# An attention and FFN kernel: two additions moved to ACT, y channel-major, deeper rings, new orders

## What is computed

```python
h = layernorm(x)
q, k, v, g = h @ Wq.T, h @ Wk.T, h @ Wv.T, h @ Wg.T          # q, k turned by RoPE, 8 heads of 16
kv, ksum, vsum = einsum(k, v), k.sum(tokens), v.sum(tokens)
num = q @ kv * scale + vsum
den = q @ ksum * scale + S                                   # S: the token count
o = (num / den + conv5(v) + conv_bias) * g                   # depthwise conv of 5 taps over tokens
x = x + o @ Wo.T
y = fp8(bf16(layernorm(x)) / s_in) @ fp8(kernel / s_k) * (s_in * s_k)
out = x + (bf16(y) + bias)                                   # y and bias in bf16
```

## Time and profile before

| what | us |
|---|---|
| median of three runs (lowest, highest) | 173.91 (173.37, 174.36) |
| the profiled execution | 173.71 |
| its span, first instruction to last | 171.9 |
| PE busy | 153.9 |
| DVE busy | 150.1 |
| POOL busy | 136.3 |
| ACT busy | 126.3 |

### The profile page before, as it was taken

One profiled execution on the slowest core, in us unless ns is written; L12 is line 12 of the kernel. 1 busy time (PEld: TensorE's weight loads), 2 busy tenths in 40 slices (PEclk: granted clock), 3 DMA queues, 4 the chain that ended last, 5 costly groups with the idle time before them and its releaser, 6 DMA issues.

```text
span 171.9 us, 3695 instructions
## 1 busy us (share of the span) xinstructions
PE 153.9 (90%) x1052; PEld 124.9 (73%) x1052; DVE 150.1 (87%) x281; ACT 126.3 (73%) x342; POOL 136.3 (79%) x163
## 2 busy tenths in 40 slices
PE   7789999999899999979999999997999799987620
PEld 2378898877688888858887989857787587965400
DVE  2279899999999999978999999969999959999663
ACT  3757783697889888598889798856798686583851
POOL 1436988858989999969889898969499796979970
PEclk9999999999999999999999999999999999999985
DMA  4932022133133616131552552341508050323223
GB/s 126 280 84 61 4 63 80 44 63 95 31 122 95 185 31 185 34 122 34 153 124 68 144 128 74 72 131 36 123 2 214 5 129 26 97 60 93 66 64 114
DMA packets 29286, 15.74 MB, mean 92 GB/s; under 512 B 9680, under 2 KB 26960, under 8 KB 29264
## 3 DMA queue, kind: packets, MB, share of 16 engines
q1 hardware_dynamic: 28688, 15.22, 33.9%
q10 hardware_dynamic: 576, 0.26, 0.6%
HBM read 5.25 MB, written 4.19 MB: 55 GB/s over the span
## 4 chain that ended last, share of the span: by engine, by line
DVE 23%; PE 22%; DMA 17%; issue 14%; POOL 10%; SPq 7%; ACT 5%; DVEq 0%; POOLq 0%; ACTq 0%
DMA xs<-_attn_hidden_states_dram 6%; DVE acc L995 6%; DMA h2T<-h 5%; DMA q_swapped<-q_turned 5%; DVE k_turned L980 4%; PE bank L1305 4%; DVE x L1047 3%; PE bank L1287 3%; DMA w_raw<-in_L_attn_Wo_dram 3%; POOL rs L671 3%; PE bank L1279 3%; DVE st L958 2%; ACT h L451 2%; PE bank L1269 2%; POOL ob L730 2%
## 5 line engine op out<-in xcount | busy, mean ns | idle before, releaser
L995 DVE SCALAR_TENSOR_TENSOR acc<-bank,conv_w,acc 128x510 f32<-128x510 f32 (+1 forms) x48 | 34.7, 722 | 0.1
L393 ACT ACTIVATE h<-xs,nmr,rs 128x128 f32<-128x128 f32 x64 | 26.3, 483 | 1.7 <-POOL nmr L663 1.5
L451 ACT ACTIVATE h<-x,nmr,rs 128x128 bf16<-128x128 f32 x60 | 24.7, 482 | 3.9 <-POOL nmr L674 3.3
L660 POOL TENSOR_TENSOR rs<-ve,minus_half 128x4 f32<-128x4 f32 (+1 forms) x17 | 16.7, 981 | 10.0 <-ACT ve L384 10.0
L671 POOL TENSOR_TENSOR rs<-ve,minus_half 128x4 f32<-128x4 f32 (+1 forms) x17 | 16.6, 978 | 8.7 <-ACT ve L442 8.6
L700 POOL TENSOR_TENSOR qT<-q_turned,q_swapped 128x512 f32<-128x512 f32 x16 | 20.4, 1277 | 3.4 <-DMA q_swapped<-q_turned 3.4
L1343 PEld LDWEIGHTS bank<-w_o,oT 128*128 128x128 f32 x128 | 16.3, 191 | 7.8 <-issue 4.0
L707 POOL TENSOR_TENSOR k<-k_turned 128x512 f32<-128x512 f32 x16 | 20.4, 1275 | 1.8 <-DVE k_turned L980 1.8
L716 POOL TENSOR_TENSOR acc<-acc,outer 128x508 f32<-128x508 f32 x16 | 20.3, 1271 | 0.6 <-DVE acc L995 0.6
L980 DVE TENSOR_TENSOR k_turned<-bank,turn_k 128x1024 f32<-128x1024 f32 x16 | 19.5, 1218 | 1.3 <-PE bank L1269 1.3
L1305 PEld LDWEIGHTS bank<-v,k 128*128 128x128 f32 x128 | 16.6, 190 | 4.4 <-issue 2.9
(11 more groups left out here) (90 smaller groups left out, 338.3 us busy)
## 6 DMA issues: line engine op xcount, KB each, us to landing
q_swapped<-q_turned SPq DMA_DIRECT2D x32, 128.0 KB, 2.8
xs<-_attn_hidden_states_dram SPq DMA_DIRECT2D x15, 256.0 KB, 3.2
out_dram<-ob SPq DMA_DIRECT2D x15, 256.0 KB, 2.9
xs<-_attn_hidden_states_dram SPq DMA_DIRECT2D x2, 128.0 KB, 2.8
turn_q<-in_turn_q_dram SPq DMA_DIRECT2D x1, 256.0 KB, 4.1
turn_k<-in_turn_k_dram SPq DMA_DIRECT2D x1, 256.0 KB, 4.3
out_dram<-ob SPq DMA_DIRECT2D x2, 128.0 KB, 1.8
h2T<-h SPq DMA_TRANSPOSE x14, 2.4
```

The source lines that it names most:

```text
L393: last = nc.scalar.activation(h[:, s, t], xs[:, u % NX, t], ACT.Identity, scale=rs1[:, s, t:t + 1], bias=nmr1[:, s, t:t + 1])
L451: last = nc.scalar.activation(h2[:, s, t], x2[:, u % 3, t], ACT.Identity, scale=rs2[:, s, t:t + 1], bias=nmr2[:, s, t:t + 1])
L995: nc.vector.scalar_tensor_tensor(out=part, in0=p_vT[:, :, lo + off:hi + off], scalar=conv_w[:, k:k + 1], in1=part, op0=ALU.mult, op1=ALU.a ...
```

## The change

The parts:

1. The token count is added to the denominators on ACT (`add_tokens`, new line L461, one instruction a unit), and not on DVE, for units 0 to 14; unit 15 keeps DVE. `den` gets two buffers.
2. For units 0 to 13 the FFN's matmul is turned round: the weights `fwq` are the stationary operand and the rounded h2T the moving one, one matmul of 512 columns; y comes with channels on the partitions. ACT scales it (`move_y`, L537) and adds the bias, now one number a partition (`add_bias` on ACT, L545), and a new DMA transpose (`turn_yc`, L296, issued by SP) brings it back to tokens on the partitions for `final_sum`. POOL's `add_bias` stays for unit 14. The bias is loaded once more as a column.
3. Rings: `NX` 4 to 6; q_turned, q_swapped, k, qT, h2, h2T, ob 2 to 3; x2 3 to 4. The new ybT and ycT have two.
4. PSUM banks are given out anew, so what each PE call waits for is another's release.
5. All lists of calls are in a new order.

```diff
-NX = 4
+NX = 6
+            def turn_yc(u):
+                s = u % 2
+                sp.wait_ge(ycT_done, count(u))
+                if u >= 2:
+                    sp.wait_ge(ob_done, count(u, 2))
+                sp.dma_start(yc[:, s], ycT[:, s], transpose=True).then_inc(yc_in[s], 16)
+            def add_tokens(u):
+                act.wait_ge(num_filled, count(u))
+                if u >= 2:
+                    act.wait_ge(rden_done, count(u, 2))
+                nc.scalar.activation(den[:, u % 2], p_num[:, :, D:NW], ACT.Identity,
+                                     bias=tokens[:, 0:1]).then_inc(den_done, 1)
...
+                nc.scalar.activation(ybT[:, u % 2], p_y[:], ACT.Copy, scale=ysc[:, 0:1]).then_inc(yb_done, 1)
+
+            def add_bias(u):
+                act.wait_ge(yb_done, count(u))
...
+                nc.scalar.activation(ycT[:, u % 2], ybT[:, u % 2], ACT.Identity,
+                                     bias=fb_act[:, 0:1]).then_inc(ycT_done, 1)
...
             def final_sum(u):
                 s = u % 2
-                pool.wait_ge(yc_done, count(u))
-                pool.wait_ge(ob_free[s], 16 * (u // 2) + 16)
+                if u < POOL_Y:
+                    pool.wait_ge(yc_in[s], 16 * (u // 2 + 1))
...
             def invert(u, j=None):
                 part = part_of(j, TPU)
-                dve.wait_ge(num_filled, count_last(u, j=j))
-                nc.vector.tensor_scalar(den[:, part], p_num[:, part, D:NW], float(S), None,
-                                        ALU.add).then_inc(den_done, 1)
                 dve.wait_ge(den_done, count_last(u, j=j))
...
                 def products(q):
+                    if u < POOL_Y:
+                        last = nc.tensor.matmul(p_y[:], fwq[:], q, start=True, stop=True)
```

More of the change, by code:

```diff
@@ new lines, in _ @@
+            add_bias(0)
+            var_eps1(6)
+            norm2(2)
+            conv_outer(5)
+            conv_middle(5)
+            norm1(6)
+            move_y(1)
+            add_tokens(4)
+            move_hT(6)
+            var_eps2(3)
+            quantise_if_small(2, is_small)
+            add_bias(1)
+            move_v(6)
+            norm2(3)
+            var_eps1(7)
+            conv_outer(6)
+            conv_middle(6)
+            norm1(7)
+            quantise_if_small(3, is_small)
@@ L570, in _ @@
+            move_hT(8)
             var_eps2(5)
             move_y(4)
[L572 removed]
+            add_bias(4)
             for t in range(9, 12):
[L574 removed]
                 move_v(t - 1)
                 var_eps1(t)
+                norm2(t - 4)
+                conv_outer(t - 1)
                 conv_middle(t - 1)
[L578 removed]
+                norm1(t)
                 quantise_if_small(t - 4, is_small)
[L580 removed]
+                add_tokens(t - 2)
+                move_hT(t)
@@ L581, in _ @@
                 var_eps2(t - 3)
                 move_y(t - 4)
-                move_hT(t)
-            norm2(8)
+                add_bias(t - 4)
             move_v(11)
             var_eps1(12)
+            norm2(8)
+            norm1(12)
             conv_outer(11)
@@ L623, in _ @@
             var_eps2(12)
+            norm2(11)
+            quantise_if_small(10, is_small)
+            move_v(15)
             norm2(12)
-            move_v(15)
-            quantise_if_small(12, is_small)
+            add_tokens(14)
+            move_y(10)
+            quantise_if_small(11, is_small)
+            add_bias(10)
             conv_outer(15)
@@ L769, in _ @@
+            final_sum(1)
             sum_outer(5)
-            add_k(6)
             pow2(4)
-            add_bias(3)
-            final_sum(3)
             add_q(6)
             pow1(8)
+            final_sum(2)
+            add_k(7)
             sum_outer(6)
-            for t in range(9, 12):
-                add_k(t - 2)
+            final_sum(3)
+            pow2(5)
+            add_q(7)
+            pow1(9)
+            final_sum(4)
+            add_k(8)
+            for t in range(10, 12):
+                sum_outer(t - 3)
@@ L1465, in _ @@
+            transpose_t1(5, (t2_done, count_last(4)))
+            transpose_v(7, (tap_done[-1], count(6)))
+            project_g(5, (v_done, count(7)))
+            project_k(7, (yb_done, count(3)))
+            sum_v(6, (t1_done, count_last(5)))
+            project_o(5, (q_turned_done, count(7)))
+            attend(6)
+            transpose_h(8, (oT_done, count_last(5)))
+            ffn(4, is_small, (k_turned_done, count(7)))
+            for t in range(9, 12):
                 key_value(t - 2, (kvs_done, count(t - 3)))
-                transpose_t1(t - 3, (hT_done, count_first(t - 1)))
```

847 lines of the change are left out of this document (457 added, 390 removed).

## The result

The changed kernel takes 177.68 us (median of 4 runs, 176.42 to 179.97), the kernel before 173.64 (173.28 to 174.36) on the same chip. The longest execution, 179.97, counts as one in a slower state and is left out of the ratio, which is 1.020 (95% interval 1.012 to 1.028; the median of the other three is 177.11). I had forecast 171.4 and given 168.0 to 177.0, so both the sign and the range were wrong. The profile is of that longest execution, 2.3 us over the median; it shows where time goes, and the medians show how much. Ratios to before are given with their 95% intervals throughout.

What follows compares the result with a forecast made beforehand. PE and DVE were taken as full, with steps of 8.79 and 8.72 us. Start 46.3, ten steps 86.5 plus 3.3 of losses, tail 24.1 and end chain 9.2 gave 169.4, plus 1.8 and 0.2: 171.4 us, range 168.0 to 177.0.

Steps and rivals of the forecast that it cites:

- The start: Start to unit 5's turning of h: 46.3 us against 47.46, from two FFNs coming later and 0.68 us of waiting gone.
- The ten steps: Unit 5's to unit 15's turning of h: 86.5 us bare plus 3.3 of losses, against 92.24 before.
- 3.3 of losses: In the ten steps: 1.0 for the loop through ACT's move of hT, 1.2 a late landing, 1.1 ACT's full queue.
- SP had room: SP's queue: new transposes land in 2.4 us each with 1.2 of SP's time, which it has to spare.
- No wait of DVE for x after 60 us: Sign in the profile after: six x buffers take away the wait at 114.55 us and its like.
- 1.6 us more cover: Rounding in the steps, now behind norm1: 1.6 us more cover for the transpose, which takes 2.4 to 4.1.
- ACT's full queue: Loss in the ten steps: between 0 and 4.75 us, taken as 1.1 because three buffers let ACT run ahead.
- The end: From unit 15's turning: 24.1 us to the last variance, then an unchanged 9.2 end chain.
- My rival in which POOL's sums give the gain back: Tail: POOL's sums of units 11 and 12 delay the last powers; 2.5 us, total 173.9, no change; chance 0.16.
- ACT as the bound: Rival for the ten steps: ACT's waits stay, step 9.75 us, total 178.0, or 174.4 with half the waits; chance 0.22.
- Its first sign: Sign of ACT as the bound: turnings of h between units 5 and 12 lie 9.3 to 9.75 us apart.
- The shared port: Rival for the end: a DVE instruction held by POOL's third sum costs 0.9 us, total 172.3; chance 0.05.

Runs made afterwards that it cites:

- weights rounded early: Changed kernel with POOL's rounding of the FFN weights back behind add_q(1), not behind add_k(3): 173.92 us, ratio to before 1.0004.
- two orders more: Changed kernel, FFN weights rounded at the old place, h2 of units 2 and 8 turned ahead of y, load of x for unit 10 earlier: 171.54 us, ratio 0.987.
- h2 turned first: Changed kernel, FFN weights rounded at the old place, h2 of unit 2 turned ahead of x's load for unit 8 and y's transpose: 172.65 us, ratio 0.989.
- changed kernels of the table: Profiles of the changed kernel, the one with weights rounded early and the one with two orders more; unit 15 to end 32.1, 32.3 and 32.4 us.
- rounding late in before: Kernel before with only the rounding of the FFN weights moved behind add_k(3): 181.13 us, ratio 1.043.
- y not turned: Changed kernel without its part 2: no transpose of y, no bias on ACT, bias on POOL ahead of each final sum: 184.44 us, ratio 1.058.
- tokens on DVE: Changed kernel without its part 1, FFN weights still rounded late: token count added on DVE ahead of the reciprocal: 177.11 us, ratio 1.019.
- wait filled: Changed kernel with 13 matmuls of zeros on PE ahead of project_q(4), FFN weights still late: 176.42 us, ratio 1.011.
- part 2 in the old order: Kernel before with part 2 of the change added and nothing else moved: 184.89 us, ratio 1.058.
- before with the deeper ring: Kernel before with six x buffers in place of four and the load of x for unit 13 issued earlier: 171.55 us, ratio 0.988.

## Why the prediction was wrong

**The start: the step that failed.** I put unit 5's turning at 46.3, from three small gains, and let every other move in the head pass at no cost. The move of `round_ffn_weights` was in the diff; I asked what POOL had to spare there, not who waits for the weights and what stands behind that wait. DVE's wait for `w_ready` is in both kernels at the same place, ahead of `residual(1)`, and PE needs that residual's bank. It came at 51.49. With the call back in place it is 46.19, so the rest of the term was right. In medians this step is 3.8 us (177.68 less 173.92) of the 6.3 by which the forecast was off, or 3.2 of 5.7 without the longest execution. I had named it only in the last sentence, "if the new order of the head costs more than its 1.1 gain", without a size or a place; as a rival it would have had one: 3.8 us of POOL work ending 13 us later.

**The ten steps: mis-sized, and one wait overlooked.** Bare 86.5 and 3.3 of losses were forecast. With the weights rounded early the losses were 7.1 (93.59), with the two orders more 4.6 (91.14). They are of two kinds.

The first is single late transfers from SP's order, as before the change: h2 of unit 2 behind a load and a transpose (1.76 and 1.34 us), x of unit 10 (0.82 in the changed kernel, 1.22 with h2 turned first), and one transpose late for a cause that stays open. Three edits of SP's list took 2.45 us off the steps in the profiles and 2.4 off the medians. I had said of the transposes that SP had room, and of the deeper x ring that it takes such waits away; the ring doesn't when the load stands late in the list. "No wait of DVE for x after 60 us" was wrong (94.32, 0.82).

The second is what is left. In the profile with two orders more, eight of the ten FFN calls in the steps cost 3.3 us more than 0.23 each, as an estimate from the distances between starts around each call, and the ninth 1.6, of which 1.24 is the wait for the late transpose. Together that is about all of the 4.6. The shape isn't the cause: where the rounding had ended long before, as at 141.07 in the changed kernel, the turned-round matmul took 0.22, as forecast. In five calls a part of it is the place: I counted the rounding behind `norm1` as 1.6 us more cover for its DMA, and didn't ask who waits for the rounding. PE's FFN does, now right behind the turning, and it starts 0.26 to 0.35 us after the rounding's end. The first call also holds the reading of the small-weights value, which before stood ahead of unit 5. No run moved the rounding or the FFN alone, so this part is read from rows and not shown by an experiment.

"ACT's full queue", 1.1, was a wrong name for it. ACT was busy 136.0 us, not 139, and taking 15 small instructions from it, which in most steps stand behind the rounding, moved the time by some 0.5 to 1 us, in both directions. So the rows point to what stands ahead of the rounding in ACT's list, not to how much ACT does.

**The end: near.** Forecast 33.3, 1.1 longer than before; measured 32.1 to 32.4 in the changed kernels of the table, as long as before. My rival in which POOL's sums give the gain back didn't come about: the sum of unit 13 waited 0.86 for its y, which ended with the stores.

**The rivals.** ACT as the bound would have given 178.0, nearly the measured time, and that would have been luck. Its first sign did show: the turnings between units 5 and 12 lay 9.6 us apart on average (9.6 with the rounding early too, 9.2 with two orders more), where I had 8.9 to 9.0 for my own case. But the amount of ACT's work didn't set them, since 15 of its instructions could go with hardly a gain; as far as the rows show, the late transfers and the costlier FFN calls did. (With half of ACT's waits that rival's own sum gives 173.3; the 174.4 holds the longer tail of my forecast.) The shared port came about. DVE's `yc` of 128x256 takes 0.28 us alone and took 1.15 beside POOL's `ob`, 0.87 more (0.9 forecast):

```profile
171.92 2.26 POOL L812 TENSOR_TENSOR ob<-x,yc 128x512 f32<-128x512 f32 x2 [0.86 <-DMA yc<-ycT]
...
173.18 1.15 DVE L997 TENSOR_TENSOR yc<-yb,fb 128x256 bf16<-128x256 bf16 x1 [0.48 <-POOL ob L812]
...
174.71 0.28 DVE L997 TENSOR_TENSOR yc<-yb,fb 128x256 bf16<-128x256 bf16 x1
```

DVE's instruction ends as POOL's does (174.33 and 174.18). The Trainium skill ("SBUF — State Buffer", "Who interferes with whom") says that an instruction of DVE with two SBUF inputs contends with one of GpSimd that reads SBUF, and that the port pair they share is an exclusive lock; the trace agrees. The 0.9 didn't lengthen the end, though: DVE's last norm, 2.44 us before, now took 1.44, with one instruction of POOL beside it in place of two. And when the wait and part of the 1.15 were taken away, the stores set the end.

**The parts.** POOL at 16 us less, DVE at 147, PE's turned-round matmul at nothing where it needn't wait: as worked out, and worth little, since the steps were not bound by the sum of any engine's work.

## What to carry to other kernels

When a call moves in an engine's list, ask first who waits for its result and what stands behind that waiting instruction; the price is that of the waiter's queue, not of the mover's. This holds above all for work that is done once, in the head, which a per-step sum doesn't see; but the rounding in the steps was the same oversight, with some 0.3 us of wait a time. To find such small waits, compare the distances between starts with those of an undisturbed step: idle time hardly shows them, since a matmul's end is modelled. A part of a change and the order around it have a price together: the same edit was 7 us of gain in one order and 11 of loss in another. And before work is moved between engines to fill gaps, look whether the gaps are one late load or transpose, which a buffer and an earlier place in the queue take away.

## What the runs showed of the hardware

- An idle TensorE costs twice. In the changed kernel's longest execution a wait of 2.77 us was followed by the lower level, 6.8 us of it in all, which took 2.7 us more until unit 5; with zeros in that wait it didn't fall. It also fell in or just after waits of 4.62 us (rounding late in before; 6.8 us at the lower level) and, for 3.4 us each, of 2.80 (y not turned), 2.71 (tokens on DVE), 1.95 (wait filled, at 81.07) and 2.09 (part 2 in the old order, at 149.88). A single long wait isn't needed: with y not turned it fell for 3.4 us from 93.0, after waits of 0.98, 0.17 and 0.37 us between 89.7 and 92.3. And a wait of 2.00 us (part 2 in the old order, at 142.01) was followed by no fall, nor were those of 1.62 (the same run, at 121.39) and 1.40 (before with the deeper ring, at 124.85).
- A transpose of 128x512 bf16 within SBUF mostly lands 2.4 us after its issue when alone. Issued some 1.3 us behind another transpose it landed 3.8 to 4.9 us after its issue in some cases and 2.4 to 2.6 in others; issued 0.6 to 0.7 us behind a load of x of 256 KB, 2.8 to 5.9. One took 2.39 us to issue and 4.33 to land though the issue before it was 4 us back, and why isn't known.
- A matmul that reads what ACT has just written started 0.26 to 0.28 us after the end of ACT's instruction in five of ten steps of the changed kernel (ACT's rounding to 81.87, PE at 82.14).
